# Attention over two contexts with a feed-forward chain: shift rows written by VectorE, reciprocals kept in PSUM, VectorE steps with one SBUF operand

## The chip, the cores and the metric

One core of a Trainium2 chip runs the whole program. The metric is the device time of one execution in microseconds (us); less is better.

## What is computed

`x` is (2, 512, 512) and the context (2, 1024, 512), all f32. The parts of the reference that matter here:

```python
q = rms_norm(linear(x, q_w, q_b), norm_q_w)            # 16 heads of 32
k_img, v_img = ...                                     # from context rows 0..256
k, v = ...                                             # from context rows 257..1023
img_x = softmax(q @ k_img.T * scale) @ v_img           # each part has its own softmax
txt_x = softmax(q @ k.T * scale) @ v
x = x + linear(img_x + txt_x, o_w, o_b)
...
# feed-forward: a chain over one row per batch (agg, 4 x [norm, d1, gelu, d2], bc), then
out = x_n + sigmoid(x_n @ gate_w + gate_b) * chain_row
x = x + layer_norm(out)
```

## The kernel before

The work of the attention is cut into 16 units `u`: one half of the tokens (256 queries, `QH`), one batch and one group of four heads each. In SBUF `kst` and `qst` hold per head 96 rows: the key (query) parts of three f32r passes stacked on the partitions. Rows 96 to 99 are for the softmax's shift: `kst` has there an indicator (image key or text key) and `qst` the negated maximum of each query, split in a high and a low part, so that the matmul of the scores subtracts the maximum by itself.

A unit has eight steps `r % 8`, one chunk of 128 keys each. `make_plan` writes the order of the whole program as one list; every engine's block goes through that list and runs its own part. A step of the list is, for TensorE:

- `S2(r)`: scores of one key chunk, transposed (keys on partitions), four matmuls with the stacked rows (L748). ScalarE takes the exponential into `prob` (L999).
- `PV(r-1)`: `prob` times the values, in PSUM bank 3 (L767), and on the last three steps of a unit the column sums in bank 6 (L772). GpSimd adds `prob` of the first five chunks together beforehand (L1368, L1371).
- `S1(t)`, with `t = r + 12`: scores of one head and 128 queries of the unit after next, in a ring of PSUM banks 0 to 2 (L730), only for their maximum. VectorE reduces them: 257 image keys (L1152), the other 255 and the 512 text keys (L1154).

At `r % 8 == 4` comes the shift of a later unit. VectorE takes the smaller of two negated maxima (`maxes`, L1160), TensorE turns the 128x8 tile `negm` with two transposes into PSUM bank 7 (L791), VectorE splits it in `crow` (`shift`, L1179 and L1180), and SyncE copies `crow` with two DMAs to rows 96 to 99 of `qst` (L624). S2 of that unit starts four steps later and waits for these DMAs (`shift_loaded`).

At a unit's end ScalarE (`attn`) copies the PV bank to `pvc` (L1005) and takes reciprocals of the sums through logarithm and exponential to `rsum` (L1008, L1010). One step later VectorE (`weigh`) multiplies `pvc` by `rsum` (L1168) and adds both halves and the bias into `attT` (L1170), from which the output projection `o` (L802) is made every four units.

Bank 7 is shared by all small jobs: the shift, `o`, and from unit 8 on the feed-forward chain (`ch_*`) and the gate (`f_*`), which the plan puts in single steps between the attention's. A job waits until the engine named in `JOBS` has emptied the one before it (`open_bank`). For a shift that is the end of L1180. VectorE's own queue is in order, as are all.

## Time and profile before

| | us |
|---|---|
| median of 3 runs | 610.99 (608.13 to 612.56) |
| span of the profiled execution | 607.0 |
| TensorE busy in the span | 533.4 (88%) |
| VectorE busy | 392.7 (65%) |
| ScalarE busy | 282.7 (47%) |
| GpSimd busy | 240.7 (40%) |

The span runs from the first to the last instruction of the profiled execution, and the profile shows no time of its own for what lies around it; the median of the runs is 4.0 us longer than the span. From 0 to about 170 us the projections are made, from 172 to 560 us the attention loop runs, and behind it the last projection and the gates. Busy time of TensorE is modelled, so the time in which it sat idle ahead of a row, and what ended that, tells more than the share. A row's "idle before" names what released the engine.

### The profile page before, as it was taken

How to read it: one execution, taken by the hardware profiler on the slowest of the kernel's cores; microseconds unless marked ns; L12 is line 12 of the kernel's file. 1: busy time of each engine (PE TensorE's matmuls, PEld its weight loads, DVE VectorE, ACT ScalarE, POOL GpSimd, SP SyncE). 2: the span in 40 equal slices, each digit the busy share in tenths (PEclk: the TensorE clock that was granted, in tenths of full speed). 3: DMA queues.
4: the chain of work that ended last, by engine and by line, in shares of the span. 5: the costliest groups of instructions: out<-in, count | busy, mean ns of one | idle time of the engine just before them, and what ended most of it. 6: DMA issues, size and time to landing. Idle time of an engine off the chain costs nothing.

```text
span 607.0 us, 9796 instructions
## 1 busy us (share of the span) xinstructions
PE 533.4 (88%) x3768; PEld 325.9 (54%) x3768; DVE 392.7 (65%) x750; ACT 282.7 (47%) x504; POOL 240.7 (40%) x138
## 2 busy tenths in 40 slices
PE   2589799999978999989999988898998998999860
PEld 2478668987644555545555454454444544554320
DVE  5547886433965787558776686476565747368676
ACT  3355744552124566426565253536362443376342
POOL 0032330032024766545655533243333345467453
PEclk9988989999979999979999998899999998799976
DMA  7506667599469699927888571707061713100001
GB/s 284 169 1 242 238 248 278 171 209 313 157 165 317 146 214 239 223 88 171 204 214 214 159 170 71 170 10 163 26 146 71 170 37 109 71 1 35 17 37 52
DMA packets 56327, 91.35 MB, mean 150 GB/s; under 512 B 5316, under 2 KB 30276, under 8 KB 55768
## 3 DMA queue, kind: packets, MB, share of 16 engines
q1 hardware_dynamic: 52032, 74.93, 45.8%
q0 software_dynamic: 3184, 14.16, 7.2%
q10 hardware_dynamic: 1064, 1.63, 1.0%
q8 instruction: 30, 0.49, 0.4%
q14 instruction: 17, 0.14, 0.1%
HBM read 70.84 MB, written 19.40 MB: 149 GB/s over the span
## 4 chain that ended last, share of the span: by engine, by line
PE 70%; DVE 16%; ACT 5%; POOL 3%; issue 2%; DMA 2%; SPq 0%; POOLq 0%; ACTq 0%; DVEq 0%
PE psum L673 14%; PE psum L767 12%; PE psum L730 10%; PE psum L748 10%; PE psum L772 5%; PE psum L802 5%; DVE negt L1154 4%; PE psum L891 3%; PE psum L856 3%; PE psum L837 2%; DMA qst<-crow 1%; DVE negm L1152 1%; DVE attT L1170 1%; POOL ssum L1323 1%; POOL ssum L1321 1%
## 5 line engine op out<-in xcount | busy, mean ns | idle before, releaser
L999 ACT ACTIVATE prob<-psum 128x512 f32<-128x512 f32 x256 | 138.6, 593 | 179.9 <-PE psum L748 175.0
L1154 DVE TENSOR_REDUCE negt<-psum 128x1 f32<-128x255 f32 (+1 forms) x256 | 129.2, 545 | 0.0
L1371 POOL TENSOR_TENSOR added<-added,prob 128x1024 f32<-128x1024 f32 x48 | 114.0, 2375 | 24.4 <-ACT prob L999 19.9
L730 PE MATMUL psum<-kst,qst 96*128 96x512 f32 x256 | 100.3, 468 | 5.3 <-DVE negt L1154 5.2
L1368 POOL TENSOR_TENSOR added<-prob 128x1024 f32<-128x1024 f32 x16 | 39.5, 2466 | 158.7 <-ACT prob L999 158.7
L1152 DVE TENSOR_REDUCE negm<-psum 128x1 f32<-128x257 f32 x128 | 53.6, 418 | 74.2 <-PE psum L730 73.6
L748 PE MATMUL psum<-qst,kst 100*128 100x256 f32 x512 | 94.9, 306 | 4.7 <-DMA qst<-crow 3.4
L767 PE MATMUL psum<-prob,vring 128*32 128x256 f32 x1152 | 94.1, 411 | 1.7 <-issue 0.5
L748 PEld LDWEIGHTS psum<-qst,kst 100*128 100x128 f32 x512 | 81.8, 200 | 24.5 <-ACT prob L999 9.6
L730 PEld LDWEIGHTS psum<-kst,qst 96*128 96x128 f32 x256 | 41.4, 195 | 67.5 <-issue 39.6
L1321 POOL TENSOR_TENSOR ssum<-sq 128x512 f32<-128x512 f32 x6 | 9.5, 1585 | 110.7 <-ACT sq L964 110.7
L673 PE MATMUL psum<-tok,p_wk 128*128 128x256 f32 (+1 forms) x192 | 37.6, 351 | 1.6 <-DVE tok L1101 1.6
L767 PEld LDWEIGHTS psum<-prob,vring 128*32 128x32 f32 x1152 | 25.4, 111 | 23.8 <-issue 7.2
L772 PE MATMUL psum<-prob,ones 128*32 128x256 f32 x512 | 36.9, 383 | 0.0
L963 ACT ACTIVATE raw<-psum,colp 128x512 f32<-128x512 f32 (+2 forms) x32 | 18.7, 583 | 36.1 <-PE psum L673 28.2
L891 PE MATMUL psum<-wg,xTt 128*128 128x512 f32 x64 | 32.1, 638 | 3.1 <-ACT xTt L1036 3.1
L673 PEld LDWEIGHTS psum<-tok,p_wk 128*128 128x128 f32 x192 | 31.0, 195 | 6.7 <-ACT sq L964 1.7
L673 PE MATMUL psum<-p_wv,tok 128*128 128x512 f32 x144 | 33.7, 390 | 0.0
L673 PE MATMUL psum<-tok,p_wq 128*128 128x512 f32 x96 | 27.4, 451 | 4.9 <-DVE p_wq L1101 4.9
L802 PE MATMUL psum<-wbuf,attT 128*128 128x512 f32 x64 | 29.3, 603 | 1.0 <-DVEq L1238 0.5
L673 PEld LDWEIGHTS psum<-p_wv,tok 128*128 128x128 f32 x144 | 27.0, 188 | 5.6
L673 PEld LDWEIGHTS psum<-tok,p_wq 128*128 128x128 f32 x96 | 21.2, 223 | 10.6 <-issue 5.8
(150 smaller groups left out, 664.4 us busy)
## 6 DMA issues: line engine op xcount, KB each, us to landing
kst<-kscr SPq DMA_DIRECT2D x96, 256.0 KB, 5.4
vring<-vscr SPq DMA_DIRECT2D x16, 576.0 KB, 8.5
kscr<-hl SPq DMA_DIRECT2D x16, 512.0 KB, 3.0
d<-d POOLq DMA_DIRECT2D x8, 1024.0 KB, 8.3
qst<-qscr SPq DMA_DIRECT2D x96, 64.0 KB, 5.9
vscr<-vbuf SPq DMA_DIRECT2D x18, 256.0 KB, 3.2
raw<-ctxT SPq DMA_DIRECT2D x4, 1024.0 KB, 5.2
qscr<-hl SPq DMA_DIRECT2D x8, 512.0 KB, 3.7
```

The source lines that it names most:

```text
L673: mm = pe.matmul(ps, left(a, kc), right(b, kc), start=(kc == 0 and a + b == 0), stop=(kc == KC - 1 and a == 1))
L730: pe.matmul(psum[:, n % 3, :], qst[0:96, slot, jj, qt * P:(qt + 1) * P], kst[0:96, slot, jj, half * 512:(half + 1) * 512], start=True, sto ...
L748: mm = pe.matmul(score2[:, j * QH:(j + 1) * QH], kst[0:100, slot, jj, k0:k0 + P], qst[0:100, slot, jj, :], start=True, stop=True)
L767: mm = pe.matmul(psum[32 * j:32 * j + 32, PV_BANK, st * QH:(st + 1) * QH], vring[:, u % 2, vc, 32 * j:32 * j + 32], prob[:, r % NP, j * QH ...
L772: mm = pe.matmul(psum[32 * j:32 * j + 32, SUM_BANK, st * QH:(st + 1) * QH], ones[:, kind, :], source[:, j * QH:(j + 1) * QH], start=first, ...
L802: mm = pe.matmul(ps, attT[:, g, n * P:(n + 1) * P], wbuf[:, g, :], start=(g == 0), stop=(g == NG - 1))
L891: mm = pe.matmul(ps, xTt[:, f % 2, kc, :], wg[:, kc, :], start=(kc == 0), stop=(kc == KC - 1))
L999: act.activation(prob[:, r % NP, part], score2[:, part], ACT.Exp).then_inc(exp2_done, 1)
L1152: dve.tensor_reduce(neg, psum[:, n % 3, 0:IMG], AX.X, ALU.max, negate=True)
L1154: dve.tensor_reduce(negt[:, u % 2, qt, half, j:j + 1], psum[:, n % 3, k0:512], AX.X, ALU.max, negate=True)\
L1368: pool.tensor_tensor(added[:, :], prob[:, (r - 1) % NP, :], prob[:, r % NP, :], ALU.add).then_inc(added_done, 1)
L1371: pool.tensor_tensor(added[:, :], added[:, :], prob[:, r % NP, :], ALU.add).then_inc(added_done, 1)
```

## The change

Four edits.

1. `negt` now holds all four candidates of a query and head and is filled once with 3e38 at the start, so that a missing one never is the minimum. `maxes` makes two reductions (one for each 128 queries) that read `negt` twice over and give 16 columns instead of 8: the eight values, then the same again.
2. TensorE's shift job is an ordinary matmul of `negm` (16 columns) by the identity, with its result on partitions 96 to 111 of bank 7. VectorE copies it to `crow` (rounded to f32r) and then writes straight to `qst`, over all four query tiles of the unit in one step: `crow * lows + psum`. `lows` is 0 for the first eight rows and -1 for the last eight, so these get the low part. No DMA; SyncE's `shift` is gone. S2 waits for `shift_written`, which a nop behind that step signals. The indicator rows of `kst` are 16, each head's with ones only for its own rows, and the matmul of S2 has 112 rows instead of 100.
3. ScalarE leaves logarithm and exponential in the sums' own PSUM bank; `rsum` is gone. `pv_emptied` counts the copy alone, and TensorE's first sum of the next unit (step 5) waits for the weighing (`attn_done`).
4. `weigh` is three VectorE steps, each with one operand in PSUM and one in SBUF.

```diff
@@ load
-                            sp.dma_start(kst[96:100, slot, jj, :].bitcast(F32), ind[:, :].bitcast(F32)).then_inc(ind_placed[u // 2], 16)
+                            rows_of = slice(4 * HPG * (2 * pp + jj), 4 * HPG * (2 * pp + jj + 1))
+                            sp.dma_start(kst[96:96 + 4 * HPG, slot, jj, :].bitcast(F32), ind[rows_of, :].bitcast(F32)).then_inc(ind_placed[u // 2], 16)
@@ shift of SyncE
-            def shift(u):
-                sp.wait_ge(emptied_by['dve'], emptied(job_at[('shift', u)])[1])
-                slot = pair_slot(u, 0)[0]
-                for part in range(2):
-                    row = 96 + 2 * part
-                    sp.dma_start(qst[row:row + 2, slot:slot + 2].rearrange("s a b n -> s (a b) n").bitcast(F32),
-                                 crow[:, part, :].bitcast(F32)).then_inc(shift_loaded[u % 2], 16)
@@ TensorE
-                    pe.wait_ge(shift_loaded[u % 2], 16 * 2 * (u // 2 + 1))
+                    pe.wait_ge(shift_written, u + 1)
...
-                    mm = pe.matmul(score2[:, j * QH:(j + 1) * QH], kst[0:100, slot, jj, k0:k0 + P],
-                                   qst[0:100, slot, jj, :], start=True, stop=True)
+                    mm = pe.matmul(score2[:, j * QH:(j + 1) * QH], kst[0:96 + 4 * HPG, slot, jj, k0:k0 + P],
+                                   qst[0:96 + 4 * HPG, slot, jj, :], start=True, stop=True)
...
-                        pe.wait_ge(pv_emptied, 2 * u)
+                        pe.wait_ge(pv_emptied, u)
...
                 if c == N_ADDED:
+                    if u > 0:
+                        pe.wait_ge(attn_done, u)
...
-                    mm = pe.transpose(ps[0:8, qt * P:(qt + 1) * P], negm[:, u % 2, qt * 8:qt * 8 + 8], ident[:, :])
+                    mm = pe.matmul(ps[96:96 + 4 * HPG, qt * P:(qt + 1) * P], negm[:, u % 2, qt], ident[:, :], start=True, stop=True)
@@ attn of ScalarE
-                act.activation(r, psum[:, SUM_BANK, :], ACT.Ln).then_inc(pv_emptied, 1)
-                act.wait_ge(pv_emptied, 2 * (u + 1))
-                act.activation(r, r, ACT.Exp, scale=-1.0).then_inc(rsum_done, 1)
+                sums = psum[:, SUM_BANK, :]
+                act.activation(sums, sums, ACT.Ln).then_inc(sum_logged, 1)
+                act.wait_ge(sum_logged, u + 1)
+                act.activation(sums, sums, ACT.Exp, scale=-1.0).then_inc(rsum_done, 1)
@@ VectorE
-                both = negt[:, u % 2]
-                dve.tensor_tensor(negm[:, u % 2, :].rearrange("p (q s j) -> p q s j", q=2, s=2)[:, :, 1, :], both[:, :, 0, :], both[:, :, 1, :],
-                                  ALU.min).then_inc(negm_done, 1)
+                for qt in range(2):
+                    twice = negt[:, u % 2, qt].rearrange("p (o s) j -> p o j s", o=1).to_broadcast([P, 2, 2 * HPG, 2])
+                    ins = dve.tensor_reduce(negm[:, u % 2, qt].rearrange("p (o j) -> p o j", o=2), twice, AX.X, ALU.min)
+                ins.then_inc(negm_done, 1)
...
-                dve.tensor_tensor(pvc[:], pvc[:], rsum[:], ALU.mult).then_inc(attn_mult, 1)
-                dve.wait_ge(attn_mult, u + 1)
-                dve.scalar_tensor_tensor(attT[:, g, :], pvc[:, 0, :], vbias[:, g:g + 1], pvc[:, 1, :], ALU.add, ALU.add)\
+                dve.wait_ge(pv_emptied, u + 1)
+                first, second = psum[:, SUM_BANK, 0:QH], psum[:, SUM_BANK, QH:2 * QH]
+                dve.tensor_tensor(first, pvc[:, 0, :], first, ALU.mult).then_inc(attn_mult, 1)
+                dve.tensor_tensor(pvc[:, 1, :], pvc[:, 1, :], second, ALU.mult).then_inc(attn_mult, 1)
+                dve.wait_ge(attn_mult, 2 * (u + 1))
+                dve.scalar_tensor_tensor(attT[:, g, :], first, vbias[:, g:g + 1], pvc[:, 1, :], ALU.add, ALU.add)\
...
-                if u >= 1:
-                    dve.wait_ge(shift_loaded[(u - 1) % 2], 16 * 2 * ((u + 1) // 2))
+                slot = pair_slot(u, 0)[0]
                 dve.wait_ge(job_done, job + 1)
-                src = psum[0:8, bank_of[job], 0:QH]
-                link(dve.tensor_copy(crow[:, 0, :], src))
-                dve.tensor_tensor(crow[:, 1, :], src, crow[:, 0, :], ALU.subtract).then_inc(emptied_by['dve'], 1)
+                rows_of = slice(96, 96 + 4 * HPG)
+                src = psum[rows_of, bank_of[job], 0:QH]
+                link(dve.tensor_copy(crow[rows_of, :], src))
+                dve.scalar_tensor_tensor(qst[rows_of, slot:slot + 2].rearrange("p a b n -> p (a b) n"),
+                                         crow[rows_of, :].rearrange("p (o n) -> p o n", o=1).to_broadcast([4 * HPG, 4, QH]), lows[rows_of, 0:1],
+                                         src.rearrange("p (o n) -> p o n", o=1).to_broadcast([4 * HPG, 4, QH]), ALU.mult, ALU.add)\
+                    .then_inc(emptied_by['dve'], 1)
+                dve.wait_ge(emptied_by['dve'], emptied(job)[1])
+                dve.engine_nop().then_inc(shift_written, 1)
```

VectorE's order around the maxes and the shift of unit 2 (`negm`, `negt`: negated maxima; `crow`: the split ones). Before:

```order
L1160 TENSOR_TENSOR negm<-negt 128x2x4 [waits max_done]
L1152 TENSOR_REDUCE negm<-psum 128x1 [waits s1_done]
L1154 TENSOR_REDUCE negt<-psum 128x1
L1154 TENSOR_REDUCE negt<-psum 128x1 [waits s1_done]
L1179 CAST crow<-psum 8x256 [waits job_done,shift_loaded1]
L1180 TENSOR_TENSOR crow<-psum,crow 8x256 [waits dve_order]
L1152 TENSOR_REDUCE negm<-psum 128x1 [waits s1_done]
```

And in the changed kernel, the same place:

```order
L1156 TENSOR_REDUCE negm<-negt 128x16 [waits max_done]
L1156 TENSOR_REDUCE negm<-negt 128x16
L1147 TENSOR_REDUCE negt<-psum 128x1 [waits s1_done]
L1149 TENSOR_REDUCE negt<-psum 128x1
L1149 TENSOR_REDUCE negt<-psum 128x1 [waits s1_done]
L1178 CAST crow<-psum 16x256 [waits job_done]
L1179 SCALAR_TENSOR_TENSOR qst<-crow,lows,psum 16x1024 [waits dve_order]
L1184 ISA [waits emptied_by_dve]
L1147 TENSOR_REDUCE negt<-psum 128x1 [waits s1_done]
```

One more step in the maxes, a step of 1024 elements for one of 256, and a nop that waits for it ahead of the next reduction.

VectorE's order around the weighing of unit 0 (`pvc`: the weighted values, `attT`: the result). Before:

```order
L1154 TENSOR_REDUCE negt<-psum 128x1 [waits s1_done]
L1168 TENSOR_TENSOR pvc<-pvc,rsum 128x512 [waits rsum_done]
L1170 SCALAR_TENSOR_TENSOR attT<-pvc,vbias 128x256 [waits attn_mult]
L1152 TENSOR_REDUCE negm<-psum 128x1 [waits s1_done]
L1154 TENSOR_REDUCE negt<-psum 128x1
```

And now:

```order
L1149 TENSOR_REDUCE negt<-psum 128x1 [waits s1_done]
L1166 TENSOR_TENSOR psum<-pvc,psum 128x256 [waits pv_emptied,rsum_done]
L1167 TENSOR_TENSOR pvc<-pvc,psum 128x256
L1169 SCALAR_TENSOR_TENSOR attT<-psum,vbias,pvc 128x256 [waits attn_mult]
L1147 TENSOR_REDUCE negt<-psum 128x1 [waits s1_done]
```

Two steps became three, at the same place.

TensorE's order around the shift job of unit 1. Before:

```order
L730 MATMUL psum<-kst,qst 128x512 [waits max_done]
L791 MATMUL psum<-ident,negm 8x128 [waits negm_done,emptied_by_dve]
L791 MATMUL psum<-ident,negm 8x128
L748 MATMUL psum<-qst,kst 128x256 [waits exp2_done]
L748 MATMUL psum<-qst,kst 128x256
```

And now:

```order
L724 MATMUL psum<-kst,qst 128x512 [waits max_done]
L787 MATMUL psum<-ident,negm 16x128 [waits negm_done,emptied_by_dve]
L787 MATMUL psum<-ident,negm 16x128
L742 MATMUL psum<-qst,kst 128x256 [waits exp2_done]
L742 MATMUL psum<-qst,kst 128x256
```

The place is the same; the two rows are transposes before and ordinary matmuls now.

## Rows read from the trace of the kernel before

**Rows 1.** Windows, loop: stretch, PE, PEld, DVE, ACT, POOL busy, PEclk, DMA, GB/s

```profile
180.00:560.00 380.00, 356.52 (x3011) 194.31 (x3004) 250.92 (x523) 189.14 (x347) 188.31 (x100) 0.95 0.55 138
```

**Rows 2.** Timeline of PE: start, duration, what, idle before; first S2 of two units

```profile
173.69 1.19 PE L748 MATMUL psum<-qst,kst 100*128 100x256 f32 x4 [1.56 <-DMA qst<-crow]
...
194.92 0.74 PE L748 MATMUL psum<-qst,kst 100*128 100x256 f32 x4 [1.81 <-DMA qst<-crow]
```

**Rows 3.** Timeline of PE: gaps behind long VectorE steps

```profile
185.46 0.38 PE L791 MATMUL psum<-ident,negm 128*8 128x128 f32 x2 [0.84 <-DVE negm L1160]
...
265.21 0.38 PE L791 MATMUL psum<-ident,negm 128*8 128x128 f32 x2 [1.57 <-DVE negm L1160]
...
421.63 0.50 PE L730 MATMUL psum<-kst,qst 96*128 96x512 f32 x1 [0.93 <-DVE negt L1154]
...
449.45 1.13 PE L802 MATMUL psum<-wbuf,attT 128*128 128x512 f32 x2 [0.51 <-DVEq L1238]
...
510.04 1.08 PE L821 MATMUL psum<-wbuf,tT 128*32 128x128 f32 x32 [1.83 <-DVE tT L1214]
```

**Rows 4.** VectorE steps: ns min/median/max or mean by line, then timeline with GpSimd

```profile
L1160 DVE TENSOR_TENSOR negm<-negt x16: 166/366/1348, 167.5 to 520.9; 128x8 f32<-128x8 f32 x16
...
L1170 DVE SCALAR_TENSOR_TENSOR attT<-pvc,vbias x16: 484/485/2480, 199.2 to 559.2; 128x256 f32<-128x256 f32 x16
...
L1168 DVE TENSOR_TENSOR pvc<-pvc,rsum x16: 667/692/2852, 198.5 to 558.5; 128x512 f32<-128x512 f32 x16
...
L1135 DVE SCALAR_TENSOR_TENSOR raw<-raw,colp,rt 128x512 f32<-128x512 f32 x8 | 6.0, 745 | 0.0
...
L1180 DVE TENSOR_TENSOR crow<-psum,crow 8x256 fp32r<-8x256 f32 x16 | 6.6, 411 | 0.6
...
262.70 2.34 POOL L1371 TENSOR_TENSOR added<-added,prob 128x1024 f32<-128x1024 f32 x1 [2.83 <-ACT prob L999]
...
263.72 1.35 DVE L1160 TENSOR_TENSOR negm<-negt 128x8 f32<-128x8 f32 x1
...
417.83 2.80 POOL L1368 TENSOR_TENSOR added<-prob 128x1024 f32<-128x1024 f32 x1 [10.79 <-ACT prob L999]
...
418.45 2.46 DVE L1170 SCALAR_TENSOR_TENSOR attT<-pvc,vbias 128x256 f32<-128x256 f32 x1
```

**Rows 5.** Timeline of PE: gaps behind the shift's second step, which frees bank 7

```profile
371.11 0.43 PE L814 MATMUL psum<-ident,chx 32*128 32x32 f32 x4 [0.97 <-DVE crow L1180]
...
432.89 1.05 PE L864 MATMUL psum<-hb,sel 128*32 128x512 f32 x2 [0.60 <-DVE crow L1180]
...
464.15 1.92 PE L856 MATMUL psum<-d,hT 128*32 128x512 f32 x16 [0.51 <-DVE crow L1180]
...
491.04 0.66 PE L846 MATMUL psum<-ident,hb 128*128 128x128 f32 x4 [0.52 <-DVE crow L1180]
```

**Rows 6.** Windows of PE alone: stretch, length, busy (rows), PEclk, DMA share, GB/s

```profile
263.00:273.00 10.00, 8.29 (x50) 0.66 0.31 107
...
340.00:346.00 6.00, 4.81 (x30) 1.00 0.40 153
...
418.00:427.00 9.00, 7.32 (x49) 0.81 0.27 61
...
511.00:526.00 15.00, 14.22 (x72) 0.54 0.18 70
```

**Rows 7.** Timeline of a plain unit, VectorE and TensorE around the shift

```profile
301.98 0.38 DVE L1160 TENSOR_TENSOR negm<-negt 128x8 f32<-128x8 f32 x1
...
306.95 0.42 DVE L1152 TENSOR_REDUCE negm<-psum 128x1 f32<-128x257 f32 x1 [1.21 <-PE psum L730]
...
302.50 0.38 PE L791 MATMUL psum<-ident,negm 128*8 128x128 f32 x2
302.64 0.72 PE L748 MATMUL psum<-qst,kst 100*128 100x256 f32 x4
```

**Rows 8.** Chain of waits: start, duration, what; one output projection

```profile
251.92 3.63 PE psum L802 x8
```

More of the change, by code:

```diff
@@ L449, in build @@
         negm_done = sem("negm_done")
-        shift_loaded = [sem(f"shift_loaded{i}") for i in range(2)]
+        shift_written = sem("shift_written")
         s2_done = sem("s2_done")
@@ L637, in f_out @@
                   .then_inc(out_stored, 16)
-            steps = {'split': split, 'norm': norm, 'vstore': vstore, 'load': load, 'load_v': load_v, 'phase2': phase2, 'shift': shift,
+            steps = {'split': split, 'norm': norm, 'vstore': vstore, 'load': load, 'load_v': load_v, 'phase2': phase2,
                      'ch_row': ch_row, 'f_out': f_out}
@@ L905, in _ @@
         def _(act):
[L906 removed]
+            for dst, src in ((ident[:, :], T['ident']), (colp[:], T['cols']), (ind_in[:, :], T['ind']), (lows[:, :], T['lows'])):
                 act.dma_start(dst, src).then_inc(const_loaded, 16)
@@ L1428 @@
     eye = np.eye(P, dtype=np.float32)
-    ind = np.zeros((4, KEYS), np.float32)
-    ind[0::2, :IMG] = 1
-    ind[1::2, IMG:] = 1
+    ind = np.zeros((HPG, 2, 2, HPG, KEYS), np.float32)
+    for j in range(HPG):
+        ind[j, :, 0, j, :IMG] = 1
+        ind[j, :, 1, j, IMG:] = 1
+    ind = ind.reshape(4 * 4 * HPG, KEYS)
+    lows = np.zeros((P, 1), np.float32)
+    lows[96 + 2 * HPG:96 + 4 * HPG] = -1
     host = {
@@ L1442 @@
         'd1_b': get('L0_ffn_d1_b'),
-        'ident': eye, 'ind': ind, 'sel': np.tile(eye[:32, :32], (4, 1)),
+        'ident': eye, 'ind': ind, 'lows': lows, 'sel': np.tile(eye[:32, :32], (4, 1)),
     }
```

25 lines of the change are left out of this document (12 added, 13 removed).

## The prediction

> **What bounds the kernel now.** I read the windows view by stage first. In the attention loop, from 180 to 560 us, TensorE is busy 356.5 of 380 us [rows 1]; VectorE, ScalarE and GpSimd each have a third or more of it free. So a change to VectorE's steps counts only where TensorE waits for one. Next I listed the gaps ahead of TensorE's own rows in the timeline, and set beside them what VectorE and GpSimd did then.
>
> The gaps that this change touches are of three kinds. (a) Two in which S2 waits for the shift rows' DMA, 1.56 us before the loop's first S2 and 1.81 us before unit 1's [rows 2]. (b) Gaps behind a VectorE step that lasts far longer than its work: 0.84, 1.57, 0.93, 0.51 and 1.83 us [rows 3]. The maxes step L1160 lasts 166 ns at best and 1348 at worst, the weighing step L1170 484 and 2480 [rows 4]. The timeline shows why: the 1.35 us one at 263.72 ends at 265.07, where the GpSimd addition that began at 262.70 ends (265.04); the 2.46 us one at 418.45 ends 0.28 us behind the GpSimd addition that ended at 420.63 [rows 4]. Both steps read two SBUF operands. (c) Gaps in which a small job waits for PSUM bank 7, which the shift's second VectorE step gives free: 0.97, 0.60, 0.51 and 0.52 us [rows 5].
>
> A rule of the Trainium skill says this too (SBUF — State Buffer, section "Who interferes with whom"): a VectorE instruction with two SBUF inputs and a GpSimd one that reads SBUF exclude each other for the whole instruction, whoever starts first. The trace agrees, with the ends above, 30 ns apart in the one case.
>
> TensorE's clock matters too. It is granted at 0.66 of full in 263:273, at 0.81 in 418:427 and at 0.54 in 511:526, each right behind a gap of kind (b); in 340:346, with TensorE busy only 4.81 of 6 us, it stayed at 1.00 [rows 6]. With 1.2 GHz as the lower of two levels these are 10 x 0.34 x 2 = 6.8 us, 9 x 0.19 x 2 = 3.4 us and 15 x 0.46 x 2 = 13.8 us at half clock. In a stage where TensorE is always busy, half of that is lost: 3.4, 1.7 and 6.9 us, 12.0 in all.
>
> **The change part by part.** The sum is made against the execution's span, 607.0 us; the median of the runs shown is 611.0, so 4.0 us lie around the span, and I take them as unchanged.
>
> *The shift rows without a DMA.* The first S2 started at 173.69 us after a gap of 1.56 [rows 2], so TensorE was through with the S1 matmuls before it at 172.13. These wait for reductions that stand behind the shift on VectorE, and the new shift step is 0.86 us longer (below), so S2 can start at about 173.0: 0.7 us won. Unit 1's S2 could follow the work before it at once: 1.8 us won. In the other 14 units the DMA was hidden behind four steps of the loop and its going wins nothing. The loads queued behind it on SyncE wait for S2 of an older unit anyway. Sum: 2.5 us.
>
> *The new shift step on VectorE.* Instead of a 256-element step of 0.41 us (L1180) there is a scalar_tensor_tensor that writes 1024 elements per partition, straight into the four query tiles. Steps of that kind took 484 ns with 256 elements and 745 with 512 [rows 4], so 1.02 ns an element, and 1024 cost 0.48 + 768 x 1.02 = 1.27 us. Bounds: 0.41 (if the repeated source came free) and 2.48 (the longest step of that kind). That is 0.86 us more in each unit. In a plain unit this is hidden: VectorE sat idle 1.21 us before the second reduction behind it [rows 7]. But the new step still reads bank 7, so whoever waits for the bank waits 0.86 us longer, four times [rows 5]: 3.4 us lost. The wait added before the nop that signals S2 holds up only reductions that come next, by that step's end, which is in the figure already.
>
> *The maxes step.* One step with two SBUF operands becomes two reductions with one each, of 16 elements read twice. Nearest rows: 166 ns for the old step unhindered, 411 for a step of 256 elements (L1180) [rows 4]; the pair lies between 0.33 and 0.82 us and I take 0.40, since what is left of so small a step is its fixed part. Ahead of TensorE's shift jobs this wins 0.84 us at 185 and about 0.95 of the 1.57 at 265 (263.72 + 0.40, plus 0.15 to TensorE). In a plain unit the old step took 0.38 us as well, and TensorE came just behind it [rows 7], so nothing changes. Where the old step ran unhindered at 0.17 and TensorE waits right behind it, 0.23 is lost; I take three such units, 0.6 us. Sum: 1.2 won.
>
> *The weighing.* A 512-element and a 256-element step become two of 256 with one operand in PSUM and one of 256: 0.41 + 0.41 + 0.48 = 1.30 us against 0.69 + 0.48 = 1.17. Unhindered it is 0.13 us longer, which only the last one, ahead of the last output projection, puts on the path. In exchange the three cases of 2.5 us go, and with them the gaps of 0.93, 0.51 and 1.83 us: 3.3 won, 0.1 lost. The Trainium skill (VectorE: DVE Perf Modes, section "Rules for kernel authors") advises against this trade: one should lower the number of chained VectorE operations. By that rule two steps more per unit are a loss of their fixed parts; the trace agrees that they cost, but against the old steps as they mostly ran it is some 0.15 us a unit, which TensorE's work covers.
>
> *ScalarE in PSUM.* Logarithm and exponential of the sums keep their size, 128x512, and only change where they write. The sum bank is now held until the weighing ends, and TensorE waits for that at its sixth step of the unit, four steps behind the weighing, some 8 us: no cost. The PV bank comes free one logarithm sooner, for which no gap in the trace waited. Both: zero, and if S2's exponentials came later by a ScalarE wait for VectorE it would show ahead of L999.
>
> *TensorE's side of the shift.* This is what the short description doesn't say. The two 128-column transposes of the 128x8 tile become two ordinary f32 matmuls with 16 weight columns. The pair of transposes took TensorE 0.14 us, from 302.50 to where S2 begins at 302.64 [rows 7]. An ordinary f32 matmul is two instructions in this trace, and eight of 512 columns took 3.63 us [rows 8]: 0.91 us a matmul, so 0.227 for 128 columns and 0.45 for the pair. That is 0.31 us more in an engine that is full, in each of 16 units: 5.0 us lost. Bounds: nothing (if a matmul by the identity cost what the transpose did) and 16 x 0.62 (all at half clock). I take 5.0.
>
> The Trainium skill says the same of the ratio (FP8 and Floating Point Precision, section "TensorE Precision Notes"): true FP32 goes through the array in four passes. By that the pair would cost four times 2 x 53 ns = 0.43 us. The trace agrees: 512 columns in 0.91 us.
>
> *Constants.* One more small load ahead of the first transposes (a column of 128 numbers) and an indicator of 64 rows instead of 4. Those transposes also wait for the statistics of the inputs, which need their own larger load first. Twelve DMAs of 64 KB instead of 16 to the keys' rows are 0.6 MB more, ahead of the loop. Zero; if the small load landed last, its delay would stand ahead of the first transposes.
>
> **The direct sum.** Won 2.5 + 1.8 (maxes) + 3.3 = 7.6; lost 3.4 (bank 7) + 0.6 + 0.1 + 5.0 = 9.1. TensorE's own rows lose 1.5 us. **The clock** decides the sign: the three gaps by the falls shrink from 1.57 to 0.6 us, from 0.93 and from 1.83 to nothing. I take the first two stretches as gone, 3.4 + 1.7, and half of the third, 3.4, because smaller waits follow there; against this one new fall of 3.4 us (1.7 lost), since the bank-7 waits grow to 1.83, 1.46, 1.37 and 1.38 us. Net 6.8 won. Altogether 5.3 us: 607.0 - 5.3 = 601.7 in the span, 605.7 in the time. I say 606.
>
> **The rivals.**
> *All clock stretches go (0.20).* Then 12.0 - 1.5 = 10.5 us: 600.5. For it: in 340:346 TensorE idled 1.2 us and the clock stayed. Against: waits of other kinds, for ScalarE's GELU above all, stay where they are.
> *The matmul by identity is as cheap as the transpose (0.12).* 5.3 + 5.0 = 10.3 won: 600.7. Against it stands that all f32 matmuls of the trace come in two instructions and cost their columns.
> *Slower: the longer bank-7 waits bring the clock down (0.14).* The shift step at 1.27 us makes four waits of 1.4 to 1.8 us, just like the one of 1.83 that preceded the 13.8 us at half clock. If each of four is followed by 6.8 us at half clock, 4 x 3.4 = 13.6 are lost against 8.5 won and the 1.5: 617.6. It decides from the point where half-clock time in the loop grows instead of shrinking; a shift step nearer its upper bound, 2.5 us, adds 4 x 1.2.
> *Nothing moves (0.12).* The holds go, but TensorE's 5 us and falls at other places take it back: 611.
> *The forecast (0.42):* 606, its own range 602 to 610.
>
> A measurement of this kernel tells about 1%, 6.1 us, from no change: faster means below 604.9. Faster: 0.20 + 0.12 + 0.08 of the forecast's case = 0.40. Slower: 0.14. Within 1%: 0.46. The range goes from 597, past both fast cases, to 617, which leaves out the worst of the slow one.
>
> **What would show it.** Right: no maxes or weighing step above 0.5 us; the new shift step at 1.2 to 1.3 us; TensorE 0.45 us from its first shift matmul to the next S2; waits for bank 7 of 1.4 to 1.8 us at the chain's jobs; clock 1.00 behind the unit at 263 and the ones at 420 and 510. Wrong: shift matmuls at 0.15 us the pair, a new gap ahead of S1 in plain units (VectorE late), waits of TensorE for the sum bank, or half-clock time in the loop above the before's.

## The result, and the profile after

| | us |
|---|---|
| kernel after, median of 20 runs | 604.68 (599.63 to 611.16) |
| kernel before beside it, 20 runs | 609.64 (605.85 to 612.86) |
| ratio | 0.9931, 95% interval 0.9908 to 0.9954 |
| span of the profiled execution | 603.6 (before 607.0) |
| mean granted clock in it | 0.952 (before 0.941) |

The ratio makes it 4.2 us faster, 0.7%, which is inside the 1% that counted as no change. Each execution's time is 1.8 to 2.2 us above its own span, over all kernels of this record. Medians here and below are of all runs of a kernel, while the ratios leave out its slow ones, a few that took over 1.5% longer than its fastest. All four edits did what they say, and yet little came of it. The windows view of the loop, after (columns as in [rows 1]):

```profile
180.00:560.00 380.00, 360.07 (x3034) 195.84 (x3034) 259.05 (x554) 187.83 (x346) 189.19 (x102) 0.96 0.52 137
```

TensorE is busier than in [rows 1], 360.1 against 356.5 us, but part of that is work it did not have before. VectorE's groups by form say what its steps cost now (line, operation, count, then busy us and mean ns, idle time before them):

```profile
L1179 DVE SCALAR_TENSOR_TENSOR qst<-crow,lows,psum 16x1024 fp32r<-16x1024 f32 x16 | 20.6, 1290 | 0.6
...
L1166 DVE TENSOR_TENSOR psum<-pvc,psum 128x256 f32<-128x256 f32 x16 | 6.8, 424 | 0.4 <-ACT psum L1005 0.2
L1167 DVE TENSOR_TENSOR pvc<-pvc,psum 128x256 f32<-128x256 f32 x16 | 6.6, 412 | 0.0
...
L1169 DVE SCALAR_TENSOR_TENSOR attT<-psum,vbias,pvc 128x256 f32<-128x256 f32 x16 | 7.7, 484 | 0.6
...
L1210 DVE TENSOR_SCALAR chx<-th,cmv,crs 32x512 f32<-32x512 f32 x4 | 4.2, 1054 | 0.1
```

and one line's view, min, median and longest in ns:

```profile
L1156 DVE TENSOR_REDUCE negm<-negt x32: 173/183/190, 167.8 to 518.5; 128x16 f32<-128x32 f32 x32
```

No maxes step is above 190 ns and the weighing's last step has a mean of 484, its unhindered duration in [rows 4], so none is held any more. But the last row of the group is new to the argument. L1210 normalises the text chain's 32x512 tile, and the diff does not touch it. Before (there L1206) its four steps on `th` took 524 to 533 ns; now their mean is 1054.

TensorE's timeline shows where that ends. The rows answer to those of [rows 2, 3, 5 and 7]:

```profile
173.23 0.72 PE L724 MATMUL psum<-kst,qst 96*128 96x512 f32 x1 [2.13 <-DVE negt L1149]
...
260.81 0.60 PE L787 MATMUL psum<-ident,negm 128*16 128x128 f32 x4 [0.51 <-DVE negm L1156]
...
297.24 0.61 PE L787 MATMUL psum<-ident,negm 128*16 128x128 f32 x4
297.78 0.73 PE L742 MATMUL psum<-qst,kst 112*128 112x256 f32 x4
...
355.82 0.41 PE L810 MATMUL psum<-ident,chx 32*128 32x32 f32 x4 [1.73 <-DVE chx L1210]
...
369.32 0.63 PE L810 MATMUL psum<-ident,chx 32*128 32x32 f32 x4 [3.66 <-DVE qst L1179]
...
433.81 1.05 PE L860 MATMUL psum<-hb,sel 128*32 128x512 f32 x2 [1.20 <-DVE qst L1179]
...
465.68 1.91 PE L852 MATMUL psum<-d,hT 128*32 128x512 f32 x14 [1.12 <-DVE qst L1179]
...
493.71 0.66 PE L842 MATMUL psum<-ident,hb 128*128 128x128 f32 x4 [1.12 <-DVE qst L1179]
```

Both DMA waits of [rows 2] are gone, and so are 0.84, 0.93, 0.51 and 1.83 of [rows 3]; the 1.57 at 265 is the 0.51 at 260.81, since the same work now comes some 4.4 us sooner. In the plain unit the shift now takes TensorE 0.54 us, from 297.24 to 297.78, where it took 0.14 [rows 7]. And the wait for bank 7 at the text chain has grown from 0.97 us [rows 5] to 3.66. The timeline of VectorE and GpSimd just before it says why; first after, then before at the same place in the program:

```profile
363.59 2.63 DVE L1210 TENSOR_SCALAR chx<-th,cmv,crs 32x512 f32<-32x512 f32 x1
367.98 1.29 DVE L1179 SCALAR_TENSOR_TENSOR qst<-crow,lows,psum 16x1024 fp32r<-16x1024 f32 x1
...
363.60 2.35 POOL L1375 TENSOR_TENSOR added<-added,prob 128x1024 f32<-128x1024 f32 x1 [2.13 <-ACT prob L995]
```

```profile
368.48 0.53 DVE L1206 TENSOR_SCALAR chx<-th,cmv,crs 32x512 f32<-32x512 f32 x1
...
368.60 2.64 POOL L1371 TENSOR_TENSOR added<-added,prob 128x1024 f32<-128x1024 f32 x1 [2.59 <-ACT prob L999]
```

The normalisation and the addition start within 10 ns of each other, and this time the normalisation is the one that waits: it ends at 366.22, 0.27 us behind the addition's end at 365.95. Before, it had started 0.12 us ahead and took 0.53, and the addition took 2.64 instead of 2.35. It has only one SBUF tensor among its operands.

TensorE's windows, three stretches of [rows 6] and one around the text chain's first jobs:

```profile
263.00:273.00 10.00, 10.00 (x104) 0.88 0.68 202
...
353.00:376.00 23.00, 16.82 (x143) 0.78 0.33 95
...
418.00:427.00 9.00, 7.51 (x48) 0.81 0.24 61
511.00:526.00 15.00, 14.22 (x104) 0.77 0.19 71
```

At the first place the clock is 0.88 where it was 0.66. That window cuts the stretch, for the wait that it follows now ends at 260.81: in 258.6:268.6 the clock is 0.83, which is 3.4 us at half clock instead of 6.8. In 511:526 the time at half clock fell from 13.8 to 15 x 0.23 x 2 = 6.9 us. The one at 418 is unchanged. Around the text chain's first jobs, 23 us from 353, there are 23 x 0.22 x 2 = 10.1 us at half clock; the same jobs had a clock of 0.85 before, in 23 us from 357, which makes 6.9. Two more stretches changed that no row above shows: in 170:182, at the loop's start, the clock is 0.86 where it was 0.72 (3.4 us at half clock instead of 6.7), and behind the loop it is 0.86 in 553.6:603.6 where it was 0.83 in 556.4:607 (14.0 instead of 17.2). The levels are 1.2 and 2.4 GHz. By the mean clocks of the table the whole execution has 607.0 x 0.059 x 2 = 71.6 us of half clock before and 603.6 x 0.048 x 2 = 57.9 after, 13.7 less.

### The profile page after: what moved, and what is told of

It reads as the page before. It is cut to its first block, busy times and chain, and to the rows that moved or that the text cites. A ratio compares the mean times of both kernels' runs of the same rounds, so it can differ in the third digit from the quotient of the medians.

```text
span 603.6 us, 9876 instructions
## 1 busy us (share of the span) xinstructions
PE 533.3 (88%) x3800; PEld 326.2 (54%) x3800; DVE 401.6 (67%) x783; ACT 282.0 (47%) x504; POOL 238.8 (40%) x138
## 4 chain that ended last, share of the span: by engine, by line
PE 70%; DVE 15%; ACT 5%; POOL 4%; issue 2%; DMA 1%; ACTq 0%; POOLq 0%; DVEq 0%
PE psum L667 13%; PE psum L761 12%; PE psum L724 11%; PE psum L742 10%; PE psum L766 6%; PE psum L798 5%; DVE negt L1149 4%; PE psum L887 3%; PE psum L852 3%; PE psum L833 2%; DMA lows<-lows 1%; POOL ssum L1327 1%; POOL ssum L1325 1%; DVE qst L1179 1%; POOL ssum L1326 1%
## 5 line engine op out<-in xcount | busy, mean ns | idle before, releaser
L1372 POOL TENSOR_TENSOR added<-prob 128x1024 f32<-128x1024 f32 x16 | 38.2, 2385 | 160.3 <-ACT prob L995 160.3
L742 PE MATMUL psum<-qst,kst 112*128 112x256 f32 x512 | 93.6, 303 | 1.9 <-ACT prob L995 1.8
L742 PEld LDWEIGHTS psum<-qst,kst 112*128 112x128 f32 x512 | 80.4, 197 | 24.8 <-ACT prob L995 10.9
L1147 DVE TENSOR_REDUCE negt<-psum 128x1 f32<-128x257 f32 x128 | 53.6, 419 | 60.3 <-PE psum L724 58.8
L761 PE MATMUL psum<-prob,vring 128*32 128x256 f32 x1152 | 91.9, 402 | 0.0
```

The source lines that it names most:

```text
L742: mm = pe.matmul(score2[:, j * QH:(j + 1) * QH], kst[0:96 + 4 * HPG, slot, jj, k0:k0 + P], qst[0:96 + 4 * HPG, slot, jj, :], start=True, s ...
L761: mm = pe.matmul(psum[32 * j:32 * j + 32, PV_BANK, st * QH:(st + 1) * QH], vring[:, u % 2, vc, 32 * j:32 * j + 32], prob[:, r % NP, j * QH ...
L1147: dve.tensor_reduce(negt[:, u % 2, qt, 0, j:j + 1], psum[:, n % 3, 0:IMG], AX.X, ALU.max, negate=True)
L1372: pool.tensor_tensor(added[:, :], prob[:, (r - 1) % NP, :], prob[:, r % NP, :], ALU.add).then_inc(added_done, 1)
```

## The experiments

Twelve kernels. Where medians and ratios disagree, both are given. Each ratio is against runs of the kernel before on the same chip; the medians of before were 608.9 us beside the first four, 609.7 beside the next four, 608.0 beside e9 to e11 and 606.9 beside the last.

| kernel | median us | ratio, 95% interval |
|---|---|---|
| after | 604.7 | 0.993 (0.991 to 0.995) |
| e1, after with transposes | 599.0 | 0.981 (0.977 to 0.985) |
| e2, before with the maxes edit | 597.7 | 0.979 (0.974 to 0.984) |
| e3, before with the weighing edit | 606.1 | 0.994 (0.990 to 0.997) |
| e4, after without the weighing edit | 607.7 | 0.998 (0.995 to 1.002) |
| e5, before with maxes and weighing | 596.0 | 0.979 (0.973 to 0.984) |
| e6, before with the VectorE shift alone | 624.3 | 1.024 (1.019 to 1.030) |
| e7, e1 with the normalisation on ScalarE | 599.4 | 0.984 (0.979 to 0.990) |
| e8, e5 with the normalisation on ScalarE | 602.5 | 0.987 (0.981 to 0.993) |
| e9, after with the constant loaded late | 603.2 | one run |
| e10, hybrid | 595.5 | 0.981 (0.976 to 0.985) |
| e11, e10 with the DMA in all units | 603.9 | 0.991 (0.987 to 0.994) |
| e12, e10 with another form of the normalisation | 590.7 | 0.972 (0.967 to 0.977) |

**e1: transposes in place of the shift matmuls.** The rows of `crow` and of the constant move to partitions 0 to 15; VectorE moves them to 96 to 111 as it writes.

```diff
-                    mm = pe.matmul(ps[96:96 + 4 * HPG, qt * P:(qt + 1) * P], negm[:, u % 2, qt], ident[:, :], start=True, stop=True)
+                    mm = pe.transpose(ps[0:4 * HPG, qt * P:(qt + 1) * P], negm[:, u % 2, qt], ident[:, :])
...
-                rows_of = slice(96, 96 + 4 * HPG)
+                rows_of, to = slice(0, 4 * HPG), slice(96, 96 + 4 * HPG)
...
-                dve.scalar_tensor_tensor(qst[rows_of, slot:slot + 2].rearrange("p a b n -> p (a b) n"),
+                dve.scalar_tensor_tensor(qst[to, slot:slot + 2].rearrange("p a b n -> p (a b) n"),
```

> The changed kernel with TensorE's two shift matmuls put back to transposes (result on partitions 0 to 15 of the bank; VectorE reads there and still writes the query rows 96 to 111). Theory (the ordinary f32 matmuls cost 0.31 us more a pair in a full engine): a plain unit lasts 17.1 us again instead of 17.4, the step from the first shift row to the next S2 is 0.15 us instead of 0.54, and the time is 4 to 6 us below the changed kernel's, about 599 to 601. Rival (the longer unit comes from the wait for the maxes or the longer VectorE step): the unit stays at 17.4 us and the time at 604 to 605.

Measured: 599.0, 5.7 us below after; by the ratios it is 7.3, by the two profiles' spans 7.2. ScalarE's copies of the PV bank to `pvc`, one a unit, give the length of a plain unit: 17.43 us after, 17.00 in e1, 17.11 before. So the matmuls cost 0.43 us in each of 16 units, 6.9 us.

**e2: the maxes edit alone,** in the layout of before, as one reduction of 8x2 elements.

```diff
-                dve.tensor_tensor(negm[:, u % 2, :].rearrange("p (q s j) -> p q s j", q=2, s=2)[:, :, 1, :], both[:, :, 0, :], both[:, :, 1, :],
-                                  ALU.min).then_inc(negm_done, 1)
+                dve.tensor_reduce(negm[:, u % 2, :].rearrange("p (q s j) -> p q s j", q=2, s=2)[:, :, 1, :], both.rearrange("p q h j -> p q j h"),
+                                  AX.X, ALU.min).then_inc(negm_done, 1)
```

> The kernel before with one edit: maxes takes the smaller maximum with one reduction (one SBUF operand) instead of a two-operand step. Theory (a step with two SBUF operands waits for GpSimd): no maxes step above 0.3 us, the gaps of 0.84 and 1.57 us at 185 and 265 us shrink to under 0.6 us, 2 to 5 us less than before (605 to 608), the upper part if the half-clock stretch behind 265 us goes. Rival (the step waits for something else than GpSimd): it still lasts up to 1.3 us and the time stays at 609 to 610.

Measured: 597.7, more than the whole change and far below the expectation. At the place of the 1.57 us gap [rows 3]:

```profile
262.08 2.35 POOL L1371 TENSOR_TENSOR added<-added,prob 128x1024 f32<-128x1024 f32 x1 [2.83 <-ACT prob L999]
...
263.09 0.17 DVE L1160 TENSOR_REDUCE negm<-negt 128x8 f32<-128x16 f32 x1
...
263.41 0.38 PE L791 MATMUL psum<-ident,negm 128*8 128x128 f32 x2 [0.39 <-DVE negm L1160]
```

```profile
263.00:273.00 10.00, 9.61 (x107) 1.00 0.60 184
```

The reduction ran through the middle of GpSimd's addition in 0.17 us, the gap is 0.39, and the clock stays at 1.00 where it was 0.66 [rows 6]. In the profile, ScalarE's copies lead those of before by 0.15 us more with each plain unit, by 4.2 us more at this place (1.2 of gap, 3 of clock), and by 2.1 more at about 365; 8.0 us in the span. The profiled execution took 601.0 us, more than this kernel's median; of the 11 to 13 us of the medians and the ratio, the profile places 8.

**e3: the weighing edit alone** (weighing, logarithm and exponential in PSUM, with their semaphores, as in the diff; DMA shift and old maxes).

> The kernel before with one edit: reciprocals in the sums' PSUM bank and the weighing in three steps with one SBUF operand each; shift DMA, transposes and the two-operand maxes stay. Theory: the three weighing steps of 2.5 us go, with the gaps at 421, 449 and 510 us (3.3 us) and a part of the half-clock time there: 3 to 8 us less than before, 602 to 607. Rival (the time saved there is only given back at the next wait): within 1.5 us of before, 608 to 611.

Measured: 606.1, 2.8 us below before by the medians and 3.9 by the ratio. The gaps of 0.93, 0.51 and 1.83 us are gone, but a maxes step got in GpSimd's way:

```profile
514.20 3.67 DVE L1162 TENSOR_TENSOR negm<-negt 128x8 f32<-128x8 f32 x1
...
513.04 2.51 POOL L1335 TENSOR_TENSOR x2e<-x2e,rows 128x512 f32<-128x512 f32 x2
515.50 2.34 POOL L1376 TENSOR_TENSOR added<-added,prob 128x1024 f32<-128x1024 f32 x1
...
518.01 0.58 PE L794 MATMUL psum<-ident,negm 128*8 128x128 f32 x2 [3.25 <-DVE negm L1162]
```

It outlasted the `x2e` additions and the whole of the one behind them, which began at 515.50, 1.3 us after this step, and it ended at 517.87, 0.03 us after that one. With one victim removed, the next was exposed.

**e4: after without the weighing edit.**

> The changed kernel with the weighing and the reciprocals put back as they were before (two steps with two SBUF operands). Theory (shift by VectorE and one-operand maxes win some 6 us up to the second quarter of the loop, and TensorE's dearer shift matmuls with the longer hold of bank 7 give all of it back): 607 to 610, about the time of before. Rival (the shift edit by itself is a gain, since the DMA wait and SyncE's queue were the main cost): 604 to 606, as the whole change.

Measured: 607.7, 3.0 above after. The held weighing steps, up to 2.48 (below) and 2.86 us, are back:

```profile
L1166 DVE SCALAR_TENSOR_TENSOR attT<-pvc,vbias x16: 483/484/2483, 192.3 to 555.5; 128x256 f32<-128x256 f32 x16
```

**e5: maxes and weighing, the shift as before.**

> The kernel before with the edits of the maxes and of the weighing with its reciprocals, and with the shift rows still written by the DMA. If the VectorE shift, with its matmuls, is what the changed kernel loses by, this one beats it clearly: the maxes alone gave 597.7, the weighing alone 3.9 us less than before, together 592 to 596; its maxes steps all below 0.2 us (in the weighing alone one was held for 3.67 us, with a gap of 3.25). If the three parts only work together, it comes out at 600 or above. 594.

Measured: 596.0, 8.7 us below after. So the third part, the shift by VectorE, is a loss of 8.7 us on top of the other two. On top of the maxes alone it is 10.0 (e2 to e4). The same runs say what the weighing wins once the maxes are done: e5 is 1.7 us below e2 by the medians and nothing by the ratios (0.9788 and 0.9789, each to within 0.006). In the profiles e5 is 5.8 us quicker than e2 from unit 1's copy to unit 15's, and loses 5.5 in unit 1, where e2's clock stayed at 1.00 and its own fell.

**e6: the shift by VectorE alone;** the maxes are two steps with two SBUF operands, one for each query tile.

```diff
-                    ins = dve.tensor_reduce(negm[:, u % 2, qt].rearrange("p (o j) -> p o j", o=2), twice, AX.X, ALU.min)
+                    ins = dve.tensor_tensor(negm[:, u % 2, qt].rearrange("p (o j) -> p o j", o=2), first, second, ALU.min)
```

> The changed kernel with the maxes as tensor_tensor steps with two SBUF operands (one for each query tile) and the weighing and reciprocals of before: only the shift by VectorE, with its ordinary matmuls, is left of the change. Theory that the shift is a loss by itself: 16 x 0.4 us of TensorE and some 2 us more of waits for bank 7, less 2.2 us of DMA waits: 6 us slower than before, 615. Rival, that the shift pays for itself and the maxes step was the whole of what the parts disagree about: 609 as before. Held maxes steps of up to 3 us are expected back.

Measured: 624.3, 14.5 us slower than before and 9 above the expectation. It is not the price of the shift by itself: beside the matmuls and bank 7, this kernel meets held steps again, of 16 elements each:

```profile
L1156 DVE TENSOR_TENSOR negm<-negt x32: 160/174/2366, 165.2 to 537.6; 128x16 f32<-128x16 f32 x32
...
472.77 0.60 PE L786 MATMUL psum<-ident,negm 128*16 128x128 f32 x4 [2.48 <-DVE negm L1156]
...
505.39 1.01 PE L786 MATMUL psum<-ident,negm 128*16 128x128 f32 x4 [2.42 <-DVE negm L1156]
```

**e7 and e8: the normalisation by ScalarE,** in e1 and in e5.

```diff
-  dve.tensor_scalar(chx[:, :], src[:, :], cmv[0:32, 0:1], crs[0:32, 0:1], ALU.subtract, ALU.mult)
+  act.activation(chx[:, :], src[:, :], ACT.Identity, bias=cneg[0:32, 1:2], scale=crs[0:32, 0:1])
```

> The changed kernel with transposes in place of the shift matmuls (599.0), and with the text chain's normalisation (32x512, from SBUF to SBUF with one tensor operand) done by ScalarE instead of VectorE. Theory: that step was held behind GpSimd for 2.6 us twice, so the gaps of 1.73 at 356 us and of 3.9 at 365 us shrink to about 0.3 and 1.3, with 3.4 us at half clock less: 593. Rival: the hold moves to another VectorE step, or ScalarE's activation comes later in its queue than VectorE did: 598 to 600.

> As the maxes and weighing together, with the DMA shift, and the text chain's normalisation done by ScalarE. Theory: the wait of 1.7 us at about 356 us goes and no held step is left in the loop, 2 to 3 us less than without it, 591. Rival: no difference, since with the old shift only one of the two normalisations was held and that wait has a ScalarE wait behind it: 594.

Measured: 599.4, as e1, and 602.5, 6.5 above e5 (5.1 by the ratios) and worse than either of e8's expectations. In e7 the chain's own gap did shrink, from 3.94 to 1.05 us, but the chain's other gap only changed its name:

```profile
347.56 0.81 ACT L1014 ACTIVATE chx<-chx,cneg,crs 32x512 f32<-32x512 f32 x1
348.28 1.05 ACT L996 ACTIVATE prob<-psum 128x512 f32<-128x512 f32 x2
...
348.90 0.98 PE L743 MATMUL psum<-qst,kst 112*128 112x256 f32 x4 [1.95 <-ACT prob L996]
...
396.98 0.98 PE L743 MATMUL psum<-qst,kst 112*128 112x256 f32 x4 [1.27 <-ACT prob L996]
```

S2's exponentials stand behind the new step in ScalarE's queue, and TensorE waits for them. The rival held. In e8 there are waits of 1.94, 1.27, 0.97 and 1.31 us for `prob` at the chain's stages, where e5 has one of 1.74 for the held step. From unit 8's copy to unit 15's e8 takes 203.0 us and e5 194.4, with a granted clock of 0.92 against 0.96, which is about 17 us more at half clock. In the profiles e8's loss is there, by its new waits and the clock together.

**e9: the small constant later.** The new load `lows` stands among those that the first transposes wait for. In after's chain of waits it is one piece from 2.32 us on:

```profile
2.32 8.65 DMA lows<-lows
10.98 0.04 issue
11.02 3.69 PE psum L660 x16
```

```diff
-            for dst, src in ((ident[:, :], T['ident']), (colp[:], T['cols']), (ind_in[:, :], T['ind']), (lows[:, :], T['lows'])):
+            for dst, src in ((ident[:, :], T['ident']), (colp[:], T['cols']), (ind_in[:, :], T['ind'])):
...
+                act.dma_start(lows[:, :], T['lows']).then_inc(rows_loaded, 16)
```

> The changed kernel with the small constant (128 numbers) loaded with the rows that only the attention loop needs, and not among those that the first transposes wait for. Theory: the first transposes start at 10.45 us again instead of 11.02, and up to 0.6 us of that reaches the loop; the chain no longer begins with that load. Rival: another load of the same group then lands as late, and they stay at 11.0.

Measured: the first transposes start at 10.30 us instead of 11.02, with VectorE's `xin` as what they waited for; 603.2 us, too small a difference for one run.

**e10: hybrid.** e1 and e9, and in units 2 to 15 VectorE writes 256 elements to a tile of one copy, which a DMA of SyncE copies to the four query tiles. In units 0 and 1 it writes all four itself.

```diff
+                if u >= 2:
...
+                    dve.scalar_tensor_tensor(srow[:, :], crow[rows_of, :], lows[rows_of, 0:1], src, ALU.mult, ALU.add)\
+                        .then_inc(emptied_by['dve'], 1)
+                    return
...
+                sp.dma_start(qst[96:96 + 4 * HPG, slot:slot + 2].rearrange("s a b n -> s (a b) n").bitcast(F32),
+                             srow[:, :].rearrange("p (o n) -> p o n", o=1).to_broadcast([4 * HPG, 4, QH]).bitcast(F32)).then_inc(shift_loaded[u % 2], 16)
```

> Transposes as in the kernel that gave 599.0, the small constant late, and VectorE writes the four query tiles itself only for units 0 and 1, where S2 waited for the DMA. In the other 14 units its second step writes 256 elements (about 0.48 us instead of 1.27) to a small tile, and one DMA of SyncE copies it to the four tiles. Theory: bank 7 comes free 0.8 us sooner, so the waits of 1.4 to 3.9 us at the text chain's jobs fall by as much, and the clock with them; the opening keeps its 2 us and more over the DMA: 593 to 595, below the maxes and weighing with the old shift (596.0). Rival: the wait of 3.9 us belongs to the held normalisation and stays, the DMA lands late at one of the stages with few steps between, and it gives 597 to 599.

Measured: 595.5, level with e5. Below e1 it is by 3.5 us in the medians and by nothing in the ratios (0.9809 and 0.9811, each to within 0.0045), so that a gain over e1 is not shown. The small jobs' waits fell from 1.4 to 0.6 us, but at the chain 3.14 us stayed, as the rival said:

```profile
356.43 2.64 DVE L1230 TENSOR_SCALAR chx<-th,cmv,crs 32x512 f32<-32x512 f32 x1
...
356.43 2.35 POOL L1395 TENSOR_TENSOR added<-added,prob 128x1024 f32<-128x1024 f32 x1 [2.08 <-ACT prob L1009]
...
361.22 0.63 PE L823 MATMUL psum<-ident,chx 32*128 32x32 f32 x4 [3.14 <-DVE srow L1196]
```

The four waits sum to 4.9 us, against 8.1 in e1. But the profiles' spans differ by 2.9 us, and 2.5 of these are there at unit 0's copy, before any edit of units 2 to 15 can act. From that copy to unit 15's e10 takes 352.4 us and e1 352.8: what the waits won, the clock took back (0.96 against 0.97).

**e11: the DMA in all 16 units.**

> The same, with the DMA for all 16 units. It differs from the one before in units 0 and 1 only. Theory: the DMA waits of 1.6 to 1.8 us ahead of the first two units' S2 are back, with 3 to 10 us more at half clock behind them, so 2 to 6 us above the hybrid: 597 to 600. Rival: the DMA waits are worth only themselves or less, and both give the same.

Measured: 603.9, 8.4 above the hybrid (5.8 by the ratios), more than expected. TensorE's timeline has the two DMA waits again, the second nearly twice as long as in [rows 2]. The DMA now carries 64 KB, with 3.2 us at the median from issue to landing in the trace (2.3 to 8.8), where two of 8 KB did it before:

```profile
170.92 1.19 PE L755 MATMUL psum<-qst,kst 112*128 112x256 f32 x4 [1.31 <-DMA qst<-srow]
193.92 1.22 PE L755 MATMUL psum<-qst,kst 112*128 112x256 f32 x4 [3.33 <-DMA qst<-srow]
```

In the profiles ScalarE's copy of unit 0 comes at 189.80 in the hybrid and at 197.06 here: 7.3 us. The DMA waits sum to 4.6, the wait for VectorE ahead of them is 1.0 shorter (0.99 instead of 1.97), and the rest is of the size of the clock, granted at 0.57 in 170:182 here and at 0.86 in the hybrid (7 us more at half clock, worth half). At the end of the span 5.7 are left. So the edit of the opening, done for two units alone, is worth 6 to 8 us in this layout. That the clock's part comes from the DMA waits is likely and not shown: e12 and e6 have no such wait and were granted 0.57 in 170:182 too, while the kernels with the DMA have 0.54 to 0.72 there.

**e12: the normalisation in a form that is not held.** The hybrid, and L1231 also writes out its sum, which nobody reads.

```diff
-  dve.tensor_scalar(chx[:, :], src[:, :], cmv[0:32, 0:1], crs[0:32, 0:1], ALU.subtract, ALU.mult)
+  dve.tensor_scalar(chx[:, :], src[:, :], cmv[0:32, 0:1], crs[0:32, 0:1], ALU.subtract, ALU.mult, accum_out=cacc[0:32, 0:1])
```

> The hybrid (595.5) with the text chain's normalisation on VectorE still, from SBUF to SBUF with one tensor, but in the form that also writes out its sum. Theory: the step is held only because it takes the engine's mode with two ports; by the Trainium skill (SBUF — State Buffer, section Who interferes with whom) the form that writes out its accumulator does not have that mode. Then all six of these steps take 0.5 to 0.8 us, the gap of 3.14 us ahead of the chain's transposes at 361 us falls to about 0.7 and the one of 1.73 us at 348 us to below 1: 590 to 592. Rival: it is held for another reason, for instance the two scalar operands that it reads from SBUF: steps of 2.5 us stay, and it gives 595 to 597.

Measured: 590.7, 4.8 us below the hybrid (5.3 by the ratios) and the fastest of all. Its steps, by line and in the timeline:

```profile
L1231 DVE TENSOR_SCALAR_CACHE_REDUCE chx<-th,cmv,crs x4: 784/786/787, 357.6 to 465.7; 32x512 f32<-32x512 f32 x4
...
357.56 0.78 DVE L1231 TENSOR_SCALAR_CACHE_REDUCE chx<-th,cmv,crs 32x512 f32<-32x512 f32 x1
...
357.57 2.36 POOL L1396 TENSOR_TENSOR added<-added,prob 128x1024 f32<-128x1024 f32 x1 [0.28 <-ACT prob L1010]
...
360.51 0.63 PE L824 MATMUL psum<-ident,chx 32*128 32x32 f32 x4 [1.30 <-DVE srow L1197]
```

It starts 10 ns ahead of the addition, as in after, reads the same tensor and the same two scalar operands, and takes 0.78 us instead of 2.63. The rival (the scalar operands) fell. All six normalisations take 0.78 or 0.79 us. The free form is 0.26 us longer than the old one unhindered, 786 ns against 526, which fits a mode given up, as the theory has it; the runs show the times and not the mode. The chain's gap of 3.14 is 1.30, and the one of 1.73 is 0.32.

## Why the prediction was right, and where not

The forecast of 606 lies 1.3 us from the median. It gave 5.3 us won; 4.2 were by the ratio, 3.4 between the two profiles. Its own split into parts did not come out so well. Each part of the sum, with the clock stretches that the forecast gave it, against the runs:

| part | forecast, with its clock | measured |
|---|---|---|
| maxes | 1.2 + 3.4 = 4.6 won | 11 to 13 won (e2) |
| weighing | 3.2 + 1.7 + 3.4 = 8.3 won | 3 to 4 won (e3, e4), 0 to 2 on top of the maxes (e2 to e5) |
| shift, all terms | 2.5 - 3.4 - 5.0 - 1.7 = 7.6 lost | 8.7 lost on top of the other two (e5 to after), 14.5 alone (e6) |

So the sum is near because the maxes were taken far too small and the weighing too large: in part luck. The 4.0 us that the prediction put around the span are not there either; an execution takes 1.8 to 2.2 us more than its span, and the profiled one of before was quicker than the median of three. From the 609.6 us of before's twenty runs its 5.3 us would have led to 604.3. The two halves of the sum, by the profiles:

*The clock: right in size, by accident.* 6.8 us won were forecast; the 13.7 us less at half clock are worth half, 6.9. It came about otherwise than told. The first stretch was halved but is not gone (a wait of 0.51 us for the maxes remains), the second stayed (0.77 and 0.72 us of waits for ScalarE lie there), the third was halved as forecast, and 3.2 us more of it came where it was feared, around the longer bank-7 wait. These places give 7.1 us less at half clock, worth 3.5 and not 6.8. The other 6.5 lie where the forecast had nothing: 3.3 at the loop's start and 3.2 behind the loop, in a stage that the edits do not touch.

*The direct sum: a loss of 1.5 forecast, 3.5 measured* (the span's 3.4 won less the clock's 6.9). Term by term:

- *Shift matmuls, forecast 5.0 lost.* The pair costs 0.54 us against 0.14; 0.40 a unit in the trace and 0.43 in e1, so 6.4 to 6.9. The mechanism was right and the size was short. It was taken from the columns of long matmuls [rows 8]; what a short one may pay beside its columns was left out, which no run separates. The rival by which it costs nothing is refuted by e1.
- *Bank 7, forecast 3.4 lost.* The four waits of [rows 5], 2.60 us in sum, are 7.10: 4.5 lost. Three of them came out smaller than forecast (1.1 to 1.2 instead of 1.4 to 1.5), though the step was sized right, 1.29 against 1.27. The fourth, 3.66 instead of 1.83, is the failed step. The forecast took the held steps to be those with two SBUF tensors, and so named two. It did not ask which others of VectorE's steps could be held once their moment against GpSimd changed. The sentence of the Trainium skill that it cited (SBUF — State Buffer, section "Who interferes with whom") stands beside a second one: a one-source step in a mode with two ports takes the same pair of ports. The trace of before had it already: one of L1206's steps on `chx` took 2.58 us, beside an addition of 2.36, and TensorE's wait of 1.74 us for it was not read:

```profile
357.50 2.58 DVE L1206 TENSOR_SCALAR chx<-chx,cmv,crs 32x512 f32<-32x512 f32 x1
...
357.45 2.36 POOL L1368 TENSOR_TENSOR added<-prob 128x1024 f32<-128x1024 f32 x1 [10.05 <-ACT prob L999]
...
360.23 0.40 PE L814 MATMUL psum<-ident,chx 32*128 32x32 f32 x4 [1.74 <-DVE chx L1206]
```

- *Opening, forecast 2.5 won.* Unit 1's 1.81 us went. At the first S2 the DMA wait of 1.56, behind one of 0.92 for VectorE, became one of 2.13 for VectorE: 0.35 won, not 0.7. The shift step ran from 171.05 to 172.34, the reductions TensorE needed came right behind it, and S1 went on at 173.23. Together 2.2.
- *Maxes, forecast 1.2 won.* In after the pair takes 0.28 us, not 0.40, and the gaps of [rows 3] shrink as forecast. But e2, with one step of 0.17, shows that the old step's 0.38 us in plain units was not free: the unit is 0.15 us shorter without it. "TensorE came just behind it [rows 7], so nothing changes" was the wrong reading. A step that TensorE reaches as it ends is on the path. With what it does to the clock, this was much the largest gain, 11.2 us by the medians of e2 and 12.8 by its ratio. This is the second step that failed: a term of 1.2 us, and 4.6 with its clock.
- *Weighing, forecast 3.2 won.* The three gaps went; e3 gives 3.9 us by its ratio and e4 3.0. That is right for the gaps alone, but the forecast added 5.1 us of clock at the same places, and with these the runs give less than half of it. Alone, a new hold took some back (the 3.25 us wait in e3). The one more step a unit costs TensorE nothing that shows: with the old shift the unit is 16.92 us with it (e5) and 16.95 without (e2).
- *Constants, forecast zero.* The first transposes start 0.57 us later, 11.02 against 10.45, and wait for `lows`; in e9 they start at 10.30. "If the small load landed last" is what happened. The size is less sure: the kernels without that load ahead start at 10.21 to 10.69, those with it (after, e1, e4, e6, e7) at 10.46 to 11.20.

The rival on the slower side had the right place: a bank-7 wait that brings the clock down. It happened once, not four times. Behind the other three waits, in 434:444, 466:476 and 494:504, the granted clock is 1.00.

Where the change's gain went is thus shown by three comparisons. Maxes and weighing are worth 13 to 14 us (e5, by ratio and medians). The VectorE shift takes 8.7 us of that back (e5 to after), of which its ordinary matmuls are 5.7 by the medians and 7.3 by the ratios (e1). The rest, 1.4 to 3.0, is not shown by itself: writing 256 elements instead of 1024, with the constant loaded late, takes 3.2 us off the waits for bank 7 (e10), but no gain in time over e1 is clear of noise. What is good in that part is confined to the first two units (e11).

What stays open: how much the clock's falls vary with small shifts of the work, and what in e8's new waits brings its clock down so much. The e5 profile itself has one that e2's lacks: 0.51 in 195:209, right behind the 1.79 us DMA wait.

## What to carry to other kernels

- When a step that GpSimd holds up is removed, list all VectorE steps that take the shared ports (here the steps with two SBUF tensors and the tensor_scalar from SBUF to SBUF) and ask of each what it meets at its new moment; the hold moves until the last is gone. Changing a step's form, to one PSUM operand, a reduction or an accumulated output, won here what moving it to another engine did not (e12 against e7 and e8).
- A replacement for a DMA is worth what the units wait for it, here two of sixteen. Do it there only, and look at what the new step holds (a bank) and at what producing its input costs the full engine.
- Time each part of a bundle alone, and also with the others in place: alone the parts gave about -12, -3 and +15 us, together -4. A total close to its forecast does not vouch for the terms.

## What the runs showed of the hardware

- The hold does not go by the size of the held step. A step of 16 elements a partition with two SBUF tensors took up to 2.37 us (e6) and one of 8 elements 3.67 (e3). That one began 1.3 us ahead of the last GpSimd addition that it outlasted: having waited first did not let it in between two of them.
- A 32x512 tensor_scalar from SBUF to SBUF, one tensor operand, f32: 0.53 us alone, 2.63 us beside a GpSimd addition that starts within 10 ns of it (after, e10); the same with accumulated output 0.78 us in either case (e12), and 0.07 us for reading the accumulator. The Trainium skill (SBUF — State Buffer, section "Who interferes with whom") states both halves, and the traces of e10 and e12 agree.
- Two 128-column f32 matmuls with 16 weight columns took TensorE 0.54 us, and the same data through two transposes 0.14 (after and e1, from the first to the next S2).
- VectorE writes 16 rows from partitions 0 to 15 to partitions 96 to 111 at no cost: 1273 ns in e1 against 1290 within 96 to 111 in after.
- The new load of 128 numbers, last of four on its queue, landed 8.65 us after its issue and is what the program's first transposes waited for.
